# Half of the second pass's x2 turns taken from TensorE over DRAM to VectorE, with a new order of work in a step

## What is computed

```
h  = layernorm(x) * (1 + ca) + sa
q, k = elu(h Wq' + bq) + 1, elu(h Wk' + bk) + 1        v = h Wv' + bv      (16 heads of 32)
KV = sum over rows of k v' (per head)    Z = 1 / (q . sum over rows of k + 1e-6)
x1 = x + ga * ((q KV Z) Wo' + bo)
```

```
x2 = layernorm(x1);  h = x2 * (1 + cb) + sb;  V = h Wv' + bv
r  = V Wg' + bg      c = norm of 8 probe products per expert      s = ln(r) + sigmoid(alpha) * ln(c)
w  = softmax of the top 2 of s
out = x1 + gb * (V + sum over experts of w_e * (silu(V W1_e' + b1_e) W2_e' + b2_e))
```

## Time and profile before

| what | before |
|---|---|
| median of 3 runs | 1216.73 us |
| profiled execution, own time | 1216.84 us |
| its span (first to last instruction) | 1215.1 us |
| TensorE matmul busy | 1202.4 us, 99% |
| TensorE weight loads busy | 987.7 us, 81% |
| VectorE busy | 1001.0 us, 82% |
| ScalarE busy | 545.0 us, 45% |
| GpSimd busy | 609.1 us, 50% |
| DMA | 131.65 MB, 34.6% of 16 engines' span |

### The profile page before, as it was taken

How to read it: one execution, slowest core, us unless ns; L and a number is a source line. 1 busy time by engine, 2 the same in 40 slices (tenths; PEclk the granted TensorE clock), 3 DMA queues, 4 the chain that set the end, 5 groups by cost and what they waited for, 6 DMA issues and landing times.

```text
span 1215.1 us, 18365 instructions
## 1 busy us (share of the span) xinstructions
PE 1202.4 (99%) x5680; PEld 987.7 (81%) x5680; DVE 1001.0 (82%) x2218; ACT 545.0 (45%) x1127; POOL 609.1 (50%) x458
## 2 busy tenths in 40 slices
PE   8999999999999999999999999999999999999998
PEld 5888878787877787887778888888888888888887
DVE  6988788988889888886788888888887888888775
ACT  4455454454454545454534343443434343443432
POOL 1443433333333443444556575766657576675741
PEclk9999999999999999999999999999999999999999
DMA  6565544444343343443231322313232231322201
GB/s 225 166 192 180 159 129 143 139 138 125 111 131 107 119 129 120 124 139 112 79 96 61 96 77 81 104 53 104 63 95 88 70 105 53 105 70 88 87 19 53
DMA packets 128515, 131.65 MB, mean 108 GB/s; under 512 B 12233, under 2 KB 82289, under 8 KB 128417
## 3 DMA queue, kind: packets, MB, share of 16 engines
q1 hardware_dynamic: 128416, 130.47, 34.6%
HBM read 80.62 MB, written 49.81 MB: 107 GB/s over the span
## 4 chain that ended last, share of the span: by engine, by line
PE 85%; DVE 5%; issue 4%; ACT 3%; DMA 1%; POOL 1%; SPq 0%; POOLq 0%; DVEq 0%; ACTq 0%
PE ps L1637 26%; PE ps L1638 26%; PE ps L1644 26%; PE ps L1853 3%; PE ps L1845 1%; DMA wm_in<-in_L_wmod_dram 1%; PE ps L1745 1%; DVE zk L1306 1%; DMA q_in<-q_scratch 1%; ACT exp_k L859 1%; ACT exp_q L830 1%; DVE qf L1282 1%; ACT exp_q L832 1%; POOL cn L725 1%; ACT exp_k L861 0%
## 5 line engine op out<-in xcount | busy, mean ns | idle before, releaser
L696 POOL TENSOR_TENSOR xn_lo<-xn,xn_hi 128x512 fp32r<-128x512 f32 x64 | 85.9, 1342 | 279.6 <-ACT xn_hi L821 279.6
L725 POOL TENSOR_TENSOR cn<-c,half 128x16 f32<-128x16 f32 x32 | 104.1, 3254 | 189.8 <-DVE c L1405 189.8
L830 ACT ACTIVATE exp_q<-qf 128x512 f32<-128x512 f32 x64 | 40.5, 632 | 150.5 <-DVE qf L1282 150.3
L1637 PE MATMUL ps<-wk_hi,xT_hi 128*128 128x512 f32 x256 | 101.8, 398 | 2.3 <-ACT xT_hi L815 2.3
L1637 PE MATMUL ps<-g_hi,qT_hi 128*128 128x512 f32 x256 | 103.2, 403 | 0.1
L1637 PE MATMUL ps<-v_hi,xT_hi 128*128 128x512 f32 x256 | 103.0, 402 | 0.0
L1637 PE MATMUL ps<-k_hi,xn_hi 128*128 128x512 f32 x256 | 102.7, 401 | 0.0
L1637 PE MATMUL ps<-wq_hi,xT_hi 128*128 128x512 f32 x256 | 102.5, 400 | 0.1
L1638 PE MATMUL ps<-wq_lo,xT_hi 128*128 128x512 f32 x256 | 101.4, 396 | 0.0
L1638 PE MATMUL ps<-wk_lo,xT_hi 128*128 128x512 f32 x256 | 101.3, 396 | 0.0
L1638 PE MATMUL ps<-k_lo,xn_hi 128*128 128x512 f32 x256 | 100.6, 393 | 0.0
(11 more groups left out here) (250 smaller groups left out, 3333.8 us busy)
## 6 DMA issues: line engine op xcount, KB each, us to landing
xin<-_attn_hidden_states_dram SPq DMA_DIRECT2D x64, 256.0 KB, 3.1
q_scratch<-qf SPq DMA_DIRECT2D x64, 256.0 KB, 3.3
xin<-_attn_hidden_states_dram SPq DMA_DIRECT2D x32, 512.0 KB, 4.2
q_in<-q_scratch SPq DMA_DIRECT2D x128, 128.0 KB, 2.9
out_dram<-qf SPq DMA_DIRECT2D x64, 256.0 KB, 2.0
xn_scratch<-xn SPq DMA_DIRECT2D x62, 256.0 KB, 2.0
xq<-xn_scratch SPq DMA_DIRECT2D x248, 64.0 KB, 2.5
wm_in<-in_L_wmod_dram SPq DMA_DIRECT2D x4, 1024.0 KB, 6.1
```

The costliest lines, as they stand in the source:

```text
L696: nc.gpsimd.tensor_tensor(moved(xn_lo[:, 1 - s, :], i + 1), kept(xn[:, 1 - s, :], i + 1), moved(f32(xn_hi[:, 1 - s, :]), i + 1), ALU.subtr ...
L725: nc.gpsimd.tensor_tensor(cn[:].rearrange("p h e -> p (h e)"), c2[:].rearrange("p h e -> p (h e)"), half[:], ALU.pow).then_inc(cn_done, 1)
L830: nc.scalar.activation(exp_q[:, s, :], zq[:, s, :], ACT.Relu, scale=-1.0).then_inc(rq_done, 1)
L1637: nc.tensor.matmul(dst, ah, bh, start=start and n == 0, stop=False)
```

## The change

- Of each pair from j = 2 on, only the first tile's x2 is turned by TensorE. The second tile's x2 is written by normalised in the order of quarters, stored to a new DRAM scratch (x2_store), loaded back by four loads (x2_load) into a new buffer x2q, and turned by VectorE into the same PSUM bank (turned_x2), after x2T_low of the first tile has read it.
- TensorE's step begins with the two out products; fused and hidden work alternate behind them. turn_x2(j, 1) is gone.
- ScalarE, VectorE and GpSimd get new orders. GpSimd's q_times_ks(j+2) now waits for scaled_q(j+1), and biased_x(j+1) stands last in its step. On VectorE biased, probes and gated stand behind the residuals, and scores behind turned_x2.
- SyncE's step takes the new store and loads between the stores of results.
- The written-out end of the pass is replaced by the general step with j = 32.

The diff, cut: where whole orders change, the lines taken out are left out, since the functions above show them.

```
--- before.py
+++ after.py
...
+    x2_dram = nc.dram_tensor("x2_scratch", [T * P, D], F32, kind="Internal").ap()
...
+        x2q = sb("x2q", [P, D], F32, late)
@@ -644,6 +649,21 @@
+            def x2_store(j, h):
+                sp.wait_ge(x2_done, 2 * j + h + 1)
+                sp.dma_start(x2_dram[rows(2 * j + h), :], xn[:, h, :]).then_inc(x2_out, 16)
+            def x2_load(j, h):
+                sp.wait_ge(x2_out, 16 * (j - 1))
+                wait_count(sp, x2T_turned, j - 2)
+                for i in range(KB):
+                    sp.dma_start(x2q[DH * i:DH * (i + 1), :].rearrange("p (g f) -> p g f", f=P),
+                                 x2_dram[rows(2 * j + h), i * P:(i + 1) * P].rearrange("(g t) f -> t g f", t=DH)).then_inc(x2_back, 16)
+            def result_store(j, h):
+                sp.wait_ge(fin_done, 2 * j + h + 1)
+                sp.dma_start(ot[rows(2 * j + h), :], out_t[:, h, :]).then_inc(stored[h], 16)
             def step_b(j):
@@ -651,10 +671,14 @@
                     bx_load(j + 1)
-                for h in range(2):
-                    if live(j - 2, J):
-                        sp.wait_ge(fin_done, 2 * (j - 2) + h + 1)
-                        sp.dma_start(ot[rows((j - 2) * 2 + h), :], out_t[:, h, :]).then_inc(stored[h], 16)
+                if live(j, J):
+                    x2_store(j, 1)
+                if live(j - 2, J):
+                    result_store(j - 2, 0)
+                if live(j, J):
+                    x2_load(j, 1)
+                if live(j - 2, J):
+                    result_store(j - 2, 1)
@@ -759,21 +783,27 @@
+            probe_norms(1)
+            q_times_ks(4)
+            row_scale(2)
+            biased_x(3)
+            router_scale(1)
+            queries_low(3)
             def step_b(j):
...
                 if live(j + 2, J):
+                    pool.wait_ge(qz_done, j + 2)
                     q_times_ks(j + 2)
...
                 if live(j + 1, J):
+                    queries_low(j + 1)
+                probe_norms(j - 1)
+                router_scale(j - 1)
+                if live(j + 1, J):
                     biased_x(j + 1)
...
+            sweep_pairs(step_b, 3, J)
@@ -873,7 +903,12 @@
                 t = 2 * j + h
-                act.wait_ge(x2T_psum, t + 1)
+                if j < 2:
+                    act.wait_ge(x2T_psum, t + 1)
+                elif h == 0:
+                    act.wait_ge(x2T_psum, j + 3)
+                else:
+                    act.wait_ge(x2T_turned, j - 1)
                 wait_count(act, y_v_done, t - 1)
@@ -916,7 +951,12 @@
                                      scale=-1.0 / D).then_inc(neg_mean_done, 1)
-                wait_count(act, x2T_psum, t - 1)
+                if j < 3:
+                    wait_count(act, x2T_psum, t - 1)
+                elif h == 0:
+                    act.wait_ge(x2T_psum, j + 2)
+                else:
+                    act.wait_ge(x2_out, 16 * (j - 2))
                 act.wait_ge(neg_mean_done, t + 1)
@@ -928,7 +968,8 @@
                 act.wait_ge(shift_done, j + 1)
-                nc.scalar.activation(xn[:, h, :], x1_of(j, h), ACT.Identity, bias=shift[:, h:h + 1],
+                dst, src = (xn[:, h, :], x1_of(j, h)) if j < 2 or h == 0 else (quarters(xn[:, h, :]), natural(x1_of(j, h)))
+                nc.scalar.activation(dst, src, ACT.Identity, bias=shift[:, h:h + 1],
                                      scale=rstd[:, h:h + 1]).then_inc(x2_done, 1)
@@ -965,37 +1006,49 @@
+            x2T_high(1, 1)
+            exponentials(0)
+            den_plus_eps(3)
+            aT_high(0, 0)
+            functions(1)
+            deviations(2, 0)
+            aT_high(0, 1)
+            deviations(2, 1)
+            variances_eps(2)
+            normalised(2, 0)
+            normalised(2, 1)
+            qT_high(3, 0)
+            qT_high(3, 1)
+            den_plus_eps(4)
+            x2T_high(2, 0)
             def step_b(j):
...
+                x2T_high(j - 1, 1)
+                exponentials(j - 2)
                 if live(j, J):
                     deviations(j, 0)
...
+                aT_high(j - 2, 0)
                 if live(j, J):
...
                     variances_eps(j)
...
+                aT_high(j - 2, 1)
                 if live(j + 1, J):
                     qT_high(j + 1, 0)
+                    qT_high(j + 1, 1)
+                if live(j, J):
+                    normalised(j, 0)
+                functions(j - 1)
+                if live(j, J):
+                    normalised(j, 1)
+                if live(j + 2, J):
+                    den_plus_eps(j + 2)
                 if live(j, J):
                     x2T_high(j, 0)
...
+            sweep_pairs(step_b, 3, J)
+            exponentials(J - 1)
+            aT_high(J - 1, 0)
+            aT_high(J - 1, 1)
@@ -1375,6 +1428,12 @@
                 nc.vector.tensor_tensor(xT_lo[:, h, :], bank_x2T, f32(xT_hi[:, h, :]), ALU.subtract).then_inc(x2Tl_done, 1)
+            def turned_x2(j, h):
+                dve.wait_ge(x2_back, 64 * (j - 1))
+                dve.wait_ge(x2Tl_done, 2 * j + h)
+                nc.vector.transpose(bank_x2T.rearrange("p (j g t) -> p g j t", j=KB, g=KB),
+                                    x2q[:].rearrange("p (g j f) -> p g j f", g=KB, j=KB)).then_inc(x2T_turned, 1)
@@ -1562,61 +1621,40 @@
             variances(1)
...
             x2T_low(2, 0)
+            turned_x2(2, 1)
             scores(1)
...
             def step_b(j):
...
+                x2T_low(j - 1, 1)
+                weights(j - 2)
+                if live(j, J):
+                    residual(j, 0)
                 if live(j + 1, J):
...
                     scaled_q(j + 1)
...
+                if live(j, J):
+                    residual(j, 1)
+                aT_low(j - 2, 0)
                 if live(j + 1, J):
                     turned_q(j + 1)
...
+                biased(j - 1, 0)
+                aT_low(j - 2, 1)
+                biased(j - 1, 1)
+                probes(j - 1)
+                gated(j - 1)
+                finished(j - 2, 0)
                 if live(j + 2, J):
                     denominators(j + 2)
...
+                finished(j - 2, 1)
+                variances(j - 1)
                 if live(j, J):
                     x2T_low(j, 0)
...
+                    turned_x2(j, 1)
+                scores(j - 1)
+            sweep_pairs(step_b, 3, J)
             weights(J - 1)
...
             aT_low(J - 1, 0)
@@ -1883,38 +1921,34 @@
+            fused_product(1, 0)
+            fused_product(1, 1)
+            out_product(2, 0)
+            turn_hidden(0, 0)
+            out_product(2, 1)
+            turn_hidden(0, 1)
+            expert_product(0, 0)
+            expert_product(0, 1)
+            value_product(1, 0)
+            turn_x2(2, 0)
+            value_product(1, 1)
             def step_b(j):
...
                 if live(j, J):
                     out_product(j, 0)
...
                     out_product(j, 1)
...
+                turn_hidden(j - 2, 0)
+                fused_product(j - 1, 0)
+                turn_hidden(j - 2, 1)
+                fused_product(j - 1, 1)
+                expert_product(j - 2, 0)
+                expert_product(j - 2, 1)
+                value_product(j - 1, 0)
                 if live(j, J):
                     turn_x2(j, 0)
...
+                value_product(j - 1, 1)
+            sweep_pairs(step_b, 3, J)
             turn_hidden(J - 1, 0)
...
```

More of the change, by code:

```diff
@@ L398, in build @@
         x2T_psum = sem("x2T_psum")
+        x2T_turned = sem("x2T_turned")
+        x2_out = sem("x2_out")
+        x2_back = sem("x2_back")
         x2Th_done = sem("x2Th_done")
@@ L966, in _ @@
             qT_high(2, 1)
-            def step_b(j):
[L969 to L979, removed]
+            x2T_high(1, 1)
[13 more added lines that the diff above has]
+            x2T_high(2, 0)
+            def step_b(j):
+                x2T_high(j - 1, 1)
+                exponentials(j - 2)
                 if live(j, J):
                     deviations(j, 0)
-                if live(j - 2, J):
-                    aT_high(j - 2, 1)
+                aT_high(j - 2, 0)
                 if live(j, J):
@@ L1564, in _ @@
             variances(1)
-            qT_low(3, 0)
             x2T_low(2, 0)
+            turned_x2(2, 1)
             scores(1)
-            qT_low(3, 1)
             def step_b(j):
[L1571 to L1577, removed]
+                x2T_low(j - 1, 1)
+                weights(j - 2)
+                if live(j, J):
+                    residual(j, 0)
                 if live(j + 1, J):
@@ L1580, in step_b @@
                     scaled_q(j + 1)
-                if live(j - 1, J):
-                    probes(j - 1)
-                    gated(j - 1)
+                if live(j, J):
+                    residual(j, 1)
+                aT_low(j - 2, 0)
                 if live(j + 1, J):
                     turned_q(j + 1)
[L1586 to L1594, removed]
```

(39 more changed lines are left out.)

9 lines of the change are left out of this document (removed).

## The result

The changed kernel takes 1229.4 us (median of 4 runs, 1229.2 to 1230.0) against 1216.7 for the kernel before (1216.6 to 1216.8) in the same comparison: a ratio of 1.0105, interval 1.0088 to 1.0123. The forecast was 1228.5. The span is 1227.6 us (before 1215.1).

A forecast was written before the change was run, and what follows sets the result against it. A GpSimd-VectorE loop of 19.46 us a step was taken to bind: +3.5 start, +5.1 steps 4 to 30, -0.4 step 31, +3.3 end, +11.5 on 1216.84 gives 1228.3, say 1228.5 us; range 1210 to 1239.

The forecast's parts named there:

- TensorE's step of 18.84: Second pass: TensorE's 19.27 us step less the removed turn's 0.43, if nothing else is late.
- The loop of 19.46: Second pass: waits circling GpSimd, VectorE, GpSimd without TensorE, locks included, set a step of 19.46 us.
- X: The end of GpSimd's queries_low(j+1), from which times within one step of the loop are counted.
- TensorE's wait for finished, 0.6 a step: Each step, value_product(j-1,0) waits some 0.6 us for finished(j-2,0), which now stands behind gated(j-1).
- The start, +3.5: Waiting for pair 2's store, loads, transpose and weights, the step ends at 657.1 instead of 653.6: +3.5 us.
- The end, +3.3: Step 32 has no out products to cover the wait for weights(30): 8.8 us to probe_norms instead of 5.5.
- the DMA chain: Second half's way over DRAM at the end: store 2.0, issues 1.3, landing 2.5, transpose 0.72 us, before scores.
- the sum (1228.3): Whole kernel: start, steps and end add 11.5 us to the profiled execution's 1216.84.
- the clock: TensorE's granted clock is 1.00 in the second pass, so nothing can be won or lost by it.
- Rival 3: Steps: x2 loads land over 1.2 us later than their median, loop 20.0, +25 us, 1242; chance 0.13.
- rival 1: Steps: locks don't meet as forecast, loop below 18.84, TensorE sets the step: -5.2 us, 1211.5; chance 0.22.

The follow-up runs named there:

- experiment 1: Changed kernel with biased_x of pairs 4 to 31 adding only 64 of 512 columns: 1215.4 us, ratio 0.9985 to the kernel before.
- experiments 3 and 4: Changed kernel with TensorE turning the second half as before (3), or VectorE transposing xn itself without store and loads (4): 1228.2 and 1226.6 us.
- Experiment 9: Changed kernel with scores and weights ahead of the new transpose and biased_x two pairs ahead, after the weights: 1216.1 us, ratio 0.9991 to the kernel before.
- experiment 5: Changed kernel with scores and weights ahead of the new transpose and biased_x(j+1) waiting for weights(j-1): 1256.6 us, ratio 1.0326 to the kernel before.
- Experiment 12: Experiment 9 with the last step reordered, TensorE's first fused product before turned hidden, VectorE's biased before aT_low: 1214.2 us, ratio 0.9977 to the kernel before.

## Why the prediction was right

- **TensorE's step of 18.84.** Right: 18.87 where nothing else binds (experiment 1).
- **The loop of 19.46.** Right to 0.01 in sum, and nearly piece by piece: probe_norms 3.34 (3.34 forecast), to router_scale 1.14 (1.15), biased_x 2.42 (2.43), scores held to its end (held), gated ending 0.55 after queries_low (0.56). Experiment 1 takes one piece away and the step falls to TensorE's; 3 and 4 leave the loop and take the rest away, and nothing changes. The transpose is at X + 6.1 and, with its 0.73 ahead of scores, inside biased_x's shadow. The Trainium skill (SBUF — State Buffer, section "SBUF: two separate sides") says that a VectorE instruction with two SBUF inputs and a GpSimd instruction that reads SBUF exclude each other for the whole instruction; the trace agrees for these large tiles, but not for the power of 128x16 (last section).
- **TensorE's wait for finished, 0.6 a step.** Right: 19.46 - 18.84, and the wait is there, 0.33 on the matmuls and up to 0.8 on the weight loads. By starts, the second expert product and the value product take 5.0 us in the changed kernel and 4.4 in an undisturbed step of experiment 1.
- **The start, +3.5.** The transpose starts at 637.17 (637.4 forecast for the landing), value_product(2,0) at 650.71 (651.1). Step 4 starts at 656.8 (657.1).
- **The end, +3.3.** The stall is 3.06 (some 3 forecast), and the weights end 22.0 us after the start of step 31 (22.0 forecast), but this was in part luck. The prediction let it come by the DMA chain alone; experiments 3 and 4 have no such chain and the same stall. The other way to these weights runs from the turn of x2(31,0) on TensorE (1197.67) over x2T_high and x2T_low (ends at 1199.61) to scores, and the transpose follows it at 1199.72 without a wait for its load. Behind the stall the end costs 1.6 us more than forecast (10.4 us from the start of step 32 to probe_norms, for 8.8), while start and steps come 0.5 sooner: that makes the 1.1 by which the profiled execution (1229.4) lies above the sum (1228.3). The missing term is the clock, of which the prediction said that nothing could be won or lost by it. The busy table behind the stall:

```profile
1204.00:1206.00 2.00, 1.92 (x12) 1.93 (x13) 0.45 (x2) 0.54 (x2) 0.00 (x0) 0.82 0.00 0
1206.00:1208.00 2.00, 2.00 (x9) 1.95 (x9) 0.50 (x1) 0.29 (x1) 0.00 (x0) 0.50 0.00 0
1208.00:1210.00 2.00, 2.00 (x12) 2.00 (x12) 0.42 (x1) 0.08 (x1) 0.00 (x0) 0.82 0.00 0
```

  After TensorE stood for 3.06 us the granted clock fell to 0.5 (1.2 GHz) for some 3.4 us, and the two fused products took 2.66 and 2.52 us where they take 1.88 at 2.4 GHz: +1.4. The runs of experiments 3 and 4 fit that price: two of four in each have a mean granted clock of 1.00 and two 0.999, and the latter take 1.8 and 1.4 us longer.
- **Rival 3** (DMA late in the steps) did not come: the loads of x2 land after 2.0 us (1.8 to 3.6; 2.5 in the earlier trace rows), and in the steps between the ends the transpose hardly waits for them (2.1 us in all from 680 to 1180). It is a part of rival 1's world, though: in experiment 1 late loads cost 2.8 us in three steps.
- **Rival 1** was nearer than it looked: it needed biased_x elsewhere. Its own price, 1211.5, was too good. Experiment 1 is this world and took 1215.4. Against the sum of rival 1 its trace has a start that is 0.9 cheaper, steps that cost 3.4 more (2.8 of it in the three with late loads) and an end that costs 1.4 more, with the same stall (3.06) and the same drop of the clock (0.58 from 1190 to 1194) as in the changed kernel.

## What to carry to other kernels

Work taken from the full engine pays only down to the next loop; write that loop out instruction by instruction before the change, with the locks between VectorE and GpSimd as terms of it, and time the removed work against it. When a large GpSimd instruction is moved to free the lock, list who reads its result too: moving it one pair further ahead was worth 40 us, moving it without that cost 27. And a reordering must be tried without the offload that it came with: here the order carried 11.4 of the 12.7 us. A transfer that is late now and then costs nothing while a longer wait covers it; when that wait is removed, look at every step and not at one, as in experiment 1.

## What the runs showed of the hardware

- Who goes first: when a VectorE instruction with two inputs in SBUF is held by queries_low and GpSimd's power of 128x16 is next in the queue, VectorE goes first, and the power takes 3.34 instead of 2.90 in these steps.
- GpSimd's power of 128x16 does not hold VectorE off for its length. In the changed kernel's step 31:

```profile
1193.25 0.69 DVE L1479 SCALAR_TENSOR_TENSOR hz<-th,zf 128x512 f32<-128x512 f32 x1 [0.23 <-ACT th L941]
```

```profile
1193.10 2.90 POOL L749 TENSOR_TENSOR cn<-c,half 128x16 f32<-128x16 f32 x1 [2.23 <-DVE c L1464]
```

  The power starts first and runs for 2.90, and the two-input VectorE instruction 0.15 later takes its plain 0.69.
- What a stall of TensorE did to the granted clock in the second pass of the profiled executions: after each of the six waits of 2.58 to 3.06 us it fell to 0.5 for some 3 to 4 us; after none of 1.59 or less did it fall while TensorE was at work again. In between, from 1.75 to 2.20 us, it fell after seven and stayed at 1.00 after five. Experiment 9 at 645 to 649 shows 0.57 after a wait of 2.20; experiment 5 kept 1.00 after the same wait:

```profile
644.02 0.41 PE L1893 MATMUL ps<-ident,aw 128*128 128x128 f32 x2 [2.20 <-DVE aT_lo L1453]
```

```profile
644.00:648.00 4.00, 3.98 (x23) 3.64 (x24) 2.62 (x6) 3.85 (x10) 3.92 (x5) 1.00 0.00 0
```

  What decides it is not known. Experiment 12, whose stall in the last step is 0.71, kept 1.00 there. Where the clock fell, it cost about half as much again as the stall in the changed kernel (1.4 for 3.06).
